# A selective scan and its parameters in one block with shared buffers, and the output stored in four transfers

## The reference, cut to what matters

```
r, B, C = rmsnorm of each part of (u @ W_x.T)
dt      = softplus(r @ W_dt.T + b_dt)                  # = max(v, 0) + ln(1 + exp(-|v|))
A       = -exp(A_log)
h[t, n] = exp(dt[t] * A[n]) * h[t-1, n] + dt[t] * u[t] * B[t, n]
y[t]    = sum over n of C[t, n] * h[t, n] + D * u[t]
x       = x + (y * silu(z)) @ W_out.T
...
x       = x + scale * (h_octonion @ w_down)            # last operation; x is the output
```

## Time and profile before

| | us |
|---|---|
| median of three runs | 2661.59 (2661.2 to 2662.74) |
| the profiled execution's own time | 2658.38 |
| its span, first to last instruction | 2656.6 |
| DVE's first scan instruction starts | 2101.40 |
| the store of x is issued | 2651.89 |

### The profile page before, as it was taken

The page is one execution under the profiler, slowest core; times in us unless marked ns, Lnnn a source line. Parts: engine busy times, 40 slices in busy tenths (PEclk is TensorE's granted clock), DMA queues, the critical chain, the costliest instruction groups (busy, mean ns, idle before and its releaser), DMA issues. The chain is left out here.

```text
span 2656.6 us, 43168 instructions
## 1 busy us (share of the span) xinstructions
PE 2530.1 (95%) x17428; PEld 2321.9 (87%) x17428; DVE 1736.4 (65%) x1979; ACT 1476.5 (56%) x2613; POOL 1293.4 (49%) x933
## 2 busy tenths in 40 slices
PE   7999999999999999999999999999999599899878
PEld 6899999999999999999999999999887377654557
DVE  2276677666677766767667776677656799743473
ACT  3365566655565555666555665556534677323572
POOL 1454655475475556457456445744500698000352
PEclk9999999999999999999999999999999699899899
DMA  5410111011111101201102100100351300287200
GB/s 203 157 50 25 50 58 32 25 57 50 38 52 50 33 31 43 65 25 53 53 25 65 50 25 27 56 27 25 106 174 53 127 1 1 82 278 239 92 1 17
DMA packets 99101, 173.91 MB, mean 65 GB/s; under 512 B 8066, under 2 KB 65666, under 8 KB 96986
## 3 DMA queue, kind: packets, MB, share of 16 engines
q1 hardware_dynamic: 90586, 162.81, 18.2%
q10 hardware_dynamic: 8320, 8.39, 0.9%
HBM read 153.28 MB, written 17.89 MB: 64 GB/s over the span
## 5 line engine op out<-in xcount | busy, mean ns | idle before, releaser
L458 POOL TENSOR_TENSOR xa_pt_lo<-xs_st,xa_pt_hi 128x1024 fp32r<-128x1024 f32 x255 | 509.9, 2030 | 574.7 <-ACT xa_pt_hi L667 574.7
L54 PE MATMUL ctx_kv_ps<-ctx_wv_hi,ctx_hi 128*128 128x256 f32 (+1 forms) x1664 | 467.5, 281 | 0.0
L56 PE MATMUL ctx_kv_ps<-ctx_wv_hi,ctx_lo 128*128 128x256 f32 (+1 forms) x1664 | 466.3, 280 | 0.0
L55 PE MATMUL ctx_kv_ps<-ctx_wv_lo,ctx_hi 128*128 128x256 f32 (+1 forms) x1664 | 466.0, 280 | 0.0
L54 PE MATMUL ctx_kv_ps<-ctx_hi,ctx_wk_hi 128*128 128x402 f32 (+1 forms) x1024 | 358.3, 350 | 2.3 <-DVE xa_k_lo L769 2.3
L55 PE MATMUL ctx_kv_ps<-ctx_lo,ctx_wk_hi 128*128 128x402 f32 (+1 forms) x1024 | 354.3, 346 | 0.0
L56 PE MATMUL ctx_kv_ps<-ctx_hi,ctx_wk_lo 128*128 128x402 f32 (+1 forms) x1024 | 353.1, 345 | 0.0
L778 DVE TENSOR_TENSOR xa_v_lo<-ctx_kv_ps,xa_v_hi 128x512 fp32r<-128x512 f32 (+1 forms) x224 | 146.3, 653 | 260.1 <-ACT xa_v_hi L640 259.4
L55 PEld LDWEIGHTS ctx_kv_ps<-ctx_wv_lo,ctx_hi 128*128 128x128 f32 (+1 forms) x1664 | 307.0, 185 | 0.0
L54 PEld LDWEIGHTS ctx_kv_ps<-ctx_wv_hi,ctx_hi 128*128 128x128 f32 (+1 forms) x1664 | 305.8, 184 | 0.0
L56 PEld LDWEIGHTS ctx_kv_ps<-ctx_wv_hi,ctx_lo 128*128 128x128 f32 (+1 forms) x1664 | 305.7, 184 | 0.0
(11 more groups left out here) (450 smaller groups left out, 6218.0 us busy)
## 6 DMA issues: line engine op xcount, KB each, us to landing
ctx_raw<-in_ctx_t SPq DMA_DIRECT2D x24, 804.0 KB, 6.7
ctx_wk_raw<-in_xa_wk SPq DMA_DIRECT2D x64, 256.0 KB, 2.9
ctx_wv_raw<-in_xa_wv SPq DMA_DIRECT2D x32, 512.0 KB, 4.4
n_back<-in_ctx SPq DMA_DIRECT2D x8, 1280.0 KB, 9.3
q_raw<-in_xa_wq SPq DMA_DIRECT2D x8, 1024.0 KB, 6.1
q_scratch<-q_q_sb ACTq DMA_DIRECT2D x8, 1024.0 KB, 4.4
ctx_q_raw<-q_scratch SPq DMA_DIRECT2D x64, 128.0 KB, 2.8
o_scratch<-xa_o_sb SPq DMA_DIRECT2D x64, 128.0 KB, 1.7
```

What stands on the lines that cost most here:

```text
L54: nc.tensor.matmul(out, left[0], right[0], start=first, stop=False)
L55: nc.tensor.matmul(out, left[0], right[1], start=False, stop=False)
L56: return nc.tensor.matmul(out, left[1], right[0], start=False, stop=last)
L458: nc.gpsimd.tensor_tensor(by_chunk(pt_lo, p), scored(j, p).rearrange("p g q c -> p g c q"), by_chunk(pt_hi, p).bitcast(F32), ALU.subtract) ...
```

## The change

The two Mamba blocks become one, in the scope `ms`; the end of the first block and of its scope go. The small buffers of the parameters now lie in those of the scan: `work`, `sq` and `bc_sb` in `h_c`, `nrm`, `steps_t` and `wd` in `h_t`, `t_ps` in `y_ps` and `d_ps` in two of the three `h_ps`. Waits take the place of the block's end: each first decay of a chunk waits for its dt, PE waits for the diagonals before it turns. ACT takes exp of A_log after the second |v|, and DVE negates it after the third maximum. POOL makes `dtu` of chunk 0 alone before the first step, and that of chunk 1 after step 1. W_out is loaded behind the copies of B and C. At the end the block that stored x is gone, and SP stores each piece of x as soon as DVE has written it, inside the last layer's block.

```
 mamba_scan, ACT
+                if h == 0:
+                    act.wait_ge(dt_set, c + 1)
...
+            for c in range(DC):
+                act.wait_ge(d_full, c + 1)
+                nc.scalar.activation(dt_sb[:, c, :], d_ps[c % 4], ACT.Abs, bias=bd[:, c:c + 1]).then_inc(d_abs, 1)
+                if c == 1:
+                    act.wait_ge(scan_in, 32)
+                    nc.scalar.activation(a_sb[:, :, :], a_sb[:, :, :], ACT.Exp).then_inc(a_exp, 1)
+                if c > 0:
+                    decline(c - 1)
+            decline(DC - 1)
+            for c in range(DC):
+                act.wait_ge(e_set, c + 1)
+                nc.scalar.activation(dt_sb[:, c, :], dt_sb[:, c, :], ACT.Ln, bias=1.0).then_inc(ln_set, 1)
+            act.wait_ge(zero_set, 1)
+            act.wait_ge(a_set, 1)
+            act.wait_ge(d_read, DC)
+            for i in range(DA):
+                decay(i)
...
 POOL
-            for c in range(2):
-                pool.wait_ge(dt_set, c + 1)
-                nc.gpsimd.tensor_tensor(dtu[:, c, :], dt_sb[:, c, :], u_sb[:, c, :], ALU.mult)
+            end.then_inc(diag_pool, 1)
+            weigh(0)
+            for i in range(STEPS):
+                c, h = divmod(i, NH)
+                if h == 0:
+                    pool.wait_ge(dtu_set, c + 1)
+                if i >= DB:
+                    pool.wait_ge(h_set, i - DB + 1)
+                if c == 0:
+                    pool.wait_ge(b_in[h], 16)
+                nc.gpsimd.tensor_tensor(by_state(d_bu, i % DB), b_all[:, h * HN:(h + 1) * HN, :],
+                                        dtu[:, c % 2, :].unsqueeze(1).broadcast_to([P, HN, R]),
+                                        ALU.mult).then_inc(dbu_set, 1)
+                if h == 1 and c + 1 < DC:
+                    weigh(c + 1)
...
 DVE
+                if c == 2:
+                    dve.wait_ge(a_exp, 1)
+                    nc.vector.tensor_scalar(a_sb[:, :, :], a_sb[:, :, :], -1.0, None, ALU.mult).then_inc(a_set, 1)
             for c in range(DC):
                 dve.wait_ge(d_read, c + 1)
                 dve.wait_ge(ln_set, c + 1)
                 nc.vector.tensor_tensor(dt_sb[:, c, :], dt_sb[:, c, :], work[:, c, :], ALU.add).then_inc(dt_set, 1)
-            dve.wait_ge(a_exp, 1)
-            nc.vector.tensor_scalar(a_sb[:, :, :], a_sb[:, :, :], -1.0, None, ALU.mult)
...
 PE, ahead of the loop over the steps
+            pe.wait_ge(bc_set, 1)
+            pe.wait_ge(diag_pool, 1)
+            pe.wait_ge(diag_dve, folded_pairs(NH))
...
 octonion_ffn, SP
+            for r in range(RT):
+                sp.wait_ge(x_set, r + 1)
+                sp.dma_start(out[:, r, :], x_sb[:, r, :]).then_inc(x_out, 16)
+            sp.wait_ge(x_out, 16 * RT)
...
 perceiver
-        with nc.Block() as block:
-            @block.sync
-            def _(sp):
-                sp.dma_start(out, x_sb[:, :, :]).then_inc(x_out, 16)
-                sp.wait_ge(x_out, 16)
```

More of the change, by code:

```diff
@@ L1666, in mamba_scan @@
-def mamba_scan(nc, u_sb, gate_sb, b_all, c_diag, c_all, b_in, c_in, dt_sb, dtu, a_sb, dk, d_bu, h_c, w_out, wo_raw, ident):
+def mamba_scan(nc, ssm_sb, u_sb, gate_sb, w_dt, b_dt, a_log, d_skip, b_all, c_diag, c_all, b_in, c_in, dt_sb, dtu, a_sb, dk,
+               d_bu, h_c, bc_dram, w_out, wo_raw, ident, eps=1e-6):
     DC, R = dt_sb.shape[1:]
     NS = b_all.shape[1]
-    RT = c_diag.shape[2]
+    RT, N = ssm_sb.shape[1:]
+    RANK = N - 2 * NS
+    COPIES = 3
+    STACK = COPIES * RANK
     DB, HN, B, L = d_bu.shape[1:]
@@ L1764, in weigh @@
             def weigh(c):
-                pool.wait_ge(dbu_set, NH * (c - 1))
+                pool.wait_ge(dt_set, c + 1)
+                if c >= 2:
+                    pool.wait_ge(dbu_set, NH * (c - 1))
                 nc.gpsimd.tensor_tensor(dtu[:, c % 2, :], dt_sb[:, c, :], u_sb[:, c, :], ALU.mult).then_inc(dtu_set, 1)
             nc.gpsimd.memset(zero[:, :, :, :], 0.0).then_inc(zero_set, 1)
+            pool.wait_ge(nrm_set, COPIES + 2)
+            for h in range(NH):
+                if folded_pair(h):
+                    for n in range(HN):
+                        for r in range(RT // 2):
+                            end = diagonal(nc.gpsimd, h, n, r)
+            end.then_inc(diag_pool, 1)
+            weigh(0)
             for i in range(STEPS):
                 c, h = divmod(i, NH)
-                if h == 0 and c >= 2:
-                    pool.wait_ge(dtu_set, c - 1)
+                if h == 0:
+                    pool.wait_ge(dtu_set, c + 1)
                 if i >= DB:
@@ L1803, in _ @@
                     h = at % NH
-                    own = (h - folded_pairs(h)) * HN
+                    first = (h - folded_pairs(h)) * HN
                     dve.wait_ge(h_set, i)
@@ L1851, in outputs @@
                 end.then_inc(y_full, 1)
+            pe.wait_ge(nrm_set, COPIES + 2)
+            for r in range(RT):
+                end = nc.tensor.transpose(t_ps[:, r * P:(r + 1) * P], nrm[:, r, :], ident[:, :])
+            end.then_inc(t_full, 1)
+            pe.wait_ge(steps_set, 1)
+            pe.wait_ge(small_in, (COPIES + 1) * 16)
+            for c in range(DC):
+                if c >= 4:
+                    pe.wait_ge(d_read, c - 3)
+                ranks = slice(c % COPIES * RANK, (c % COPIES + 1) * RANK)
+                nc.tensor.matmul(d_ps[c % 4], wd[ranks, c * P:(c + 1) * P], steps_t[ranks, :], start=True,
+                                 stop=True, tile_position=(c % COPIES * RANK, 0)).then_inc(d_full, 1)
+            pe.wait_ge(bc_set, 1)
+            pe.wait_ge(diag_pool, 1)
+            pe.wait_ge(diag_dve, folded_pairs(NH))
             for i in range(STEPS + LAG):
@@ L2999, in _, with octonion_ffn @@
                     norm_out.low(dve, r)
[L3002 removed]
+def octonion_ffn(nc, x_sb, xt_hi, xt_lo, weights, out, x_out):
     RT, H = x_sb.shape[1:]
```

217 lines of the change are left out of this document (85 added, 132 removed).

## The result

The changed kernel takes 2665.86 us (median of 20 runs, 2663.38 to 2667.05) against 2661.39 for the kernel before (20 runs, 2658.94 to 2662.74). The ratio is 1.0017, with a 95% interval of 1.0011 to 1.0023: 4.5 us more, where 0.11% or 3.0 us more was forecast. The difference is clear of the noise, and it is less than the 0.2% that the prediction counts as no change.

A forecast was written before the change was run, and what follows sets the result against it. DVE bounds the scan stage, which ends a fixed time after its first scan instruction. A later scan start, +5.2, and shorter tail, -2.2, gave +3.0 us on the median 2661.59: 2664.6 us, range 2660.0 to 2668.5.

The forecast's parts named there:

- The turns: Ahead of the scan, DVE additions and POOL products alternate, each standing still for the other; first scan at 2106.6, +5.2 us.
- rival of additions that `d_bu` leaves alone: Ahead of the scan, POOL's `d_bu` doesn't hold up DVE's additions: -6.3 us in all, 2655.3 us; chance 0.12.
- rival of two additions per turn: DVE gets two additions in per POOL instruction, scan starts at 2102.3: -1.3 us in all, 2660.3 us; chance 0.06.
- The path without turns: Start of the scan if nothing got in the way: logarithms end at 2094.52, first decay ready at 2097.2.
- The tail: End of the kernel: last piece issued at 2649.6, landing in 2.0, span ending at 2654.4 for 2656.6: 2.2 us gained.
- The cold PE: Rival in the scan: low clock lasts twice as long after PE's first turn, +3.3 us, 2667.9 in all; chance 0.16.
- a clock much as before: Clause of the main forecast, chance 0.66: PE's low clock at the scan's start lasts about as before.
- a clock of 0.50 past 2118: Sign of being wrong: PE's low clock reaching past 2118, with new DVE waits in the scan for ACT or PE.
- The products that POOL made in the meantime buy nothing: In the scan, POOL's early products gain no time, because DVE was not waiting for them later on.

The follow-up runs named there:

- hold_pool: Changed kernel, but POOL waits for all eight additions before its second product `d_bu`; 2659.23 us, ratio 0.9993 to the kernel before.
- ln_psum: Changed kernel, but ACT writes the eight logarithms to PSUM, so each addition has one input there; 2655.54 us, ratio 0.998 to the kernel before.
- one_store: Changed kernel with its four stores of x as one transfer of 1024 KB inside the last block; 2668.15 us, run once.
- a_exp_early: Kernel before, still in two blocks, with the exponential of A among the others and the negation behind the third maximum; 2662.03 us, run once.
- warm_pe: Changed kernel plus twelve idle products on PE ahead of its first turn; 2666.48 us, ratio 1.0021 to the kernel before.
- warm_long: Changed kernel plus twenty-two idle products on PE, reaching up to its first turn; 2665.93 us, ratio 1.002 to the kernel before.

## Why the prediction was right, and where it was off

**The turns** (+5.2 forecast) held piece by piece. Additions 4, 5, 7 and 8 took 2.82 or 2.83, for 2.8; addition 6 took 1.75, for 1.7; the group lasted 15.65, for 15.7; the first scan came at 2106.69, for 2106.6, and waited for nobody. The forecast of 5.2 splits in two: 0.22 by which the moved exponential delays the logarithms, and 5.0 from the first addition on. The table has +0.20 and +4.93 for them, and another +0.16 from code ahead of the change. That the turns are the cause is shown twice: without POOL's stream beside them the additions are short (hold_pool), and with POOL's stream but one input in PSUM they are too (ln_psum). The rival of additions that `d_bu` leaves alone fell with the 2.83 beside each `d_bu`, and the rival of two additions per turn with the timeline, where each POOL instruction has one addition beside it.

**The path without turns** was worked out as a first decay at 2097.2; it was ready at 2097.3, and ln_psum turned that into a scan 6.26 after the first addition.

**The tail** (-2.2 forecast, -1.76 measured) was mis-sized. I took 2.0 for a piece of 256 KB between 1.7 and 3.9; it was 2.35. The ends of the block and the scopes took 5.31 - 0.03 - 2.35 = 2.93, where I had 2.8. I had allowed 0.1 for the issue and it took 0.03. The gain is in the splitting, as one_store showed; the prediction didn't separate splitting from moving.

**The cold PE**, priced as a rival at +3.3 for a clock back 7.6 us later, came true in small. The clock came back 9.1 us after the first turn instead of 7.6. The prediction's own measure, 0.93 us of full-speed work less 0.5 done in each microsecond at the low clock, gives 1.5 x 0.43 = 0.6 for that, and the scan stage grew by 0.63. All of it lies ahead of the end of DVE's wait, and other kernels bear this out:

| kernel | clock back after the first turn | first scan to the end of DVE's wait |
|---|---|---|
| before | 7.53 | 17.43 |
| a_exp_early | 8.49 | 17.77 |
| ln_psum | 8.93 | 18.02 |
| changed | 9.05 | 18.06 |
| warm_pe | 9.63 | 18.29 |
| one_store | 10.28 | 18.64 |

Both columns are in us, and the first is by the clock's own records, where the windows above are rounded. From the first row to the last that is 1.21 us for 2.75 us more of the low clock, 0.44 for each, where the measure says 0.43. (hold_pool, with 11.11 and 20.01, lies 1.0 above this line: that much is POOL's, and by an estimate at 0.44 the clock's part of its 2.0 is 0.9.) So the measure was right. The rival had tied the late clock to PE's longer rest, which the traces don't bear out (see the last section). The forecast's clause "a clock much as before" was what failed, by 0.6 us. It is a part of the prediction's own sign of being wrong: a clock of 0.50 past 2118, which came by 0.2 us, together with a wait that had grown from 1.74 to 2.63. The wait of 1.7 that the kernel before already had is likely of the same origin: warm_long, which nearly removes the changed kernel's wait, has a scan stage 1.7 us shorter than the kernel before (176.78 and 178.47). On the kernel before itself it wasn't tested.

**"The products that POOL made in the meantime buy nothing"** held in the sum. The first scans do follow each other at 2.20 and 2.18 us in place of 2.31 and 2.30, since no product is waited for, and DVE reaches the place of its wait 0.26 earlier. But the wait ends when PE has caught up, so that DVE only waits the longer: of the 0.9 that the wait grew, 0.26 are this and 0.63 the clock.

**Behind the scan** the forecast had nothing, and +0.51 and +0.35 were measured there. The first, from the last output to x (the start of its last addition), is 29.3 to 29.6 in every merged kernel whose PE began cold, 28.9 and 29.0 in the two that kept the clock up, and 28.8 to 29.1 in the kernels with two blocks; I didn't take it apart, and its cause is open. The second lies within what this stage does by itself.

In sum, the profiled executions differ by +5.0 where +3.0 was forecast: the scan's start is off by 0.1 (5.3 for 5.2), the tail by 0.4, the scan stage by 0.6, and the stages behind it by 0.9. All four lie on the same side, so no error hid another. The step that carried the sign was right, and it wasn't luck. The medians differ by +4.5, 1.5 above the forecast.

## What to carry to other kernels

When a change lets one engine's stream start earlier, look at what it now runs beside: here POOL's early products turned eight additions of 0.68 us into a group of 15.65, 9.3 us where the merging was worth 2.6, and one operand placed in PSUM turned the loss into a kernel 5.8 us faster than the one before. Count such a stage from marks inside it, not from the span or the median, because equal code ahead of it differed by up to 3.3 us and a later stage took back or gave 2 to 3 us by itself. The length of a wait isn't its price: look at when it ends. And where a program ends with a store that waits for its data, try issuing it in pieces as they are finished; here that gave 1.5 us.

## What the runs showed of the hardware that I had not expected

- The clock fell while PE was at rest, before its work began again: in warm_pe the last idle product ended at 2102.9 and the clock was 0.50 from 2107.6 on.
- The time until the clock came back after the first turn was not the same for the same turns: 7.6 us in the kernel before, 9.1 in the changed one, 8.5 in a_exp_early and 10.3 in one_store. A longer rest of PE ahead of the turns doesn't explain it: PE rested 17.15 us in the kernel before and 21.95 in the changed one, but in ln_psum it rested only 12.62 and the clock still took 8.9 us. The cause is open.
- The same instructions behind the Mamba layer ran with two low-clock stretches of 10.2 and 10.3 us in one kernel, and of 13.6 and 13.8 in another, and the stage took 3.3 us longer with them.
- A `d_bu`, which repeats one of its inputs, held a DVE addition with two SBUF inputs just as the plain `dtu` did: 2.83 us beside 2.36 us of work, and 1.75 beside 1.28.
- A logarithm written to PSUM cost ACT no more than one written to SBUF (eight in 4.27 us in the changed kernel, six in 3.19 in ln_psum), and the addition that reads it took the same 0.68.
- Four stores of 256 KB, issued 0.66 us apart, landed 2.3 us after their issue at the median, where a single one of 1024 KB took 3.9.
